# A graph layer kernel: its first matmul on row halves, its scatter on column halves, its bias copied by ScalarE

## What is computed

```python
h = relu(layernorm(x))
xp = h @ lin1_w
C = 0.5 * (cos(edge_weight * PI / 10) + 1)
W = (ssp(edge_attr @ mlp_w1 + b1) @ mlp_w2 + b2) * C[:, None]
msg = xp[src] * W
agg = segment_sum(msg, dst)
x + ssp(agg @ lin2_w + lin2_b) @ lin_w + lin_b
```

## Time and profile before

| | us |
|---|---|
| median of 3 runs | 2164.73 |
| lowest and highest run | 2164.29, 2168.45 |
| span of the profiled execution | 2162.6 |
| TensorE matmuls busy | 1804.4 |
| TensorE weight loads busy | 1331.3 |
| VectorE busy | 1433.5 |
| ScalarE busy | 636.2 |
| GpSimd busy | 1626.7 |

### The profile page before, as it was taken

One profiled execution on the slowest core, in us unless ns is written; L12 is line 12 of the kernel. 1 busy time (PEld: TensorE's weight loads), 2 busy tenths in 40 slices (PEclk: granted clock), 3 DMA queues, 4 the chain that ended last, 5 costly groups with the idle time before them and its releaser, 6 DMA issues.

```text
span 2162.6 us, 28443 instructions
## 1 busy us (share of the span) xinstructions
PE 1804.4 (83%) x8534; PEld 1331.3 (62%) x8535; DVE 1433.5 (66%) x3688; ACT 636.2 (29%) x976; POOL 1626.7 (75%) x1742
## 2 busy tenths in 40 slices
PE   6888888888877888878888888888878888878887
PEld 6556666666655656656665666666656666655665
DVE  7867666666665666666666666666667666666665
ACT  6323232222222222222232222222322223222221
POOL 7877777777777777777777777777777777777775
PEclk9678787687787787887687877777778678788776
DMA  9322222222232222223232222222222222232221
GB/s 286 90 73 69 81 76 75 79 76 81 68 82 81 71 79 81 75 74 82 68 82 79 77 79 70 81 81 68 81 81 75 74 81 76 74 81 76 73 72 47
DMA packets 100170, 175.95 MB, mean 81 GB/s; under 512 B 29163, under 2 KB 67748, under 8 KB 94870
## 3 DMA queue, kind: packets, MB, share of 16 engines
q0 software_dynamic: 53152, 108.91, 18.0%
q1 hardware_dynamic: 46868, 65.22, 11.4%
HBM read 161.21 MB, written 12.80 MB: 80 GB/s over the span
## 4 chain that ended last, share of the span: by engine, by line
POOL 60%; issue 20%; PE 14%; DMA 3%; DVE 2%; DVEq 0%; ACT 0%; POOLq 0%; SPq 0%
POOL XG L307 59%; PE PW L619 4%; PE PA L631 4%; PE PX L605 3%; DMA XG<-xp_scratch,IX 3%; PE PW L617 1%; DVE SCR L403 1%; POOL TB L207 1%; DVE XG L509 1%; PE PF L648 0%; DVE MV L409 0%; PE PF L656 0%; PE PW L586 0%; DMA X<-x 0%; PE PX L573 0%
## 5 line engine op out<-in xcount | busy, mean ns | idle before, releaser
L307 POOL DMA_INDIRECT XG<-xp_scratch,IX x1661 | 1574.8, 948 | 507.4 <-issue 498.3
L371 ACT ACTIVATE TB<-TB 128x512 f32<-128x512 f32 x416 | 261.7, 629 | 1407.0 <-DVE TB L491 1406.9
L619 PEld LDWEIGHTS PW<-W,TB 128*128 128x128 f32 x3322 | 592.2, 251 | 21.4
L619 PE MATMUL PW<-W,TB 128*128 128x128 f32 x3322 | 594.5, 338 | 0.0
L509 DVE TENSOR_TENSOR XG<-PW,XG 128x512 f32<-128x512 f32 x416 | 286.2, 688 | 451.1 <-DMA XG<-xp_scratch,IX 448.1
L605 PE MATMUL PX<-AT,W 50*128 50x512 f32 x832 | 554.8, 752 | 7.1 <-DMA AT<-attr_t 7.1
L631 PEld LDWEIGHTS PA<-OH,XG 128*128 128x128 f32 x3322 | 544.4, 248 | 1.0 <-DVE XG L509 0.5
L631 PE MATMUL PA<-OH,XG 128*128 128x64 f32 x3322 | 543.3, 322 | 0.2 <-DVE AG L517 0.2
L617 PEld LDWEIGHTS PW<-BPB,ones 128*128 128x128 bf16 x416 | 41.3, 99 | 704.4 <-issue 649.6
L617 PE MATMUL PW<-BPB,ones 128*128 128x512 bf16 x416 | 195.2, 469 | 315.4 <-DVE XG L509 314.4
L491 DVE TENSOR_SCALAR TB<-PX,B 128x512 f32<-128x512 f32 x416 | 309.8, 745 | 202.9 <-PE PX L605 200.5
(11 more groups left out here) (73 smaller groups left out, 329.2 us busy)
## 6 DMA issues: line engine op xcount, KB each, us to landing
AT<-attr_t SPq DMA_DIRECT2D x103, 400.0 KB
XG<-xp_scratch,IX POOLq DMA_INDIRECT x1661, 2.5
X<-x SPq DMA_DIRECT2D x12, 512.0 KB, 7.4
xp_scratch<-XG SPq DMA_DIRECT2D x24, 256.0 KB, 4.4
out<-X SPq DMA_DIRECT2D x24, 256.0 KB, 5.2
IX<-src_t SPq DMA_DIRECT2D x1, 830.5 KB, 6.5
CC<-ew_t SPq DMA_DIRECT2D x1, 830.5 KB, 8.4
DI<-dst_t SPq DMA_DIRECT2D x1, 830.5 KB
```

The costliest lines, as they stand in the source:

```text
L307: e.indirect_dma_start(XG[q % XG_N][0:p, k * D:(k + 1) * D], None, xp, bass.IndirectOffsetOnAxis(ap=IX[0:p, t0 + k:t0 + k + 1], axis=0)).t ...
L371: e.activation(T[:, 0:w], T[:, 0:w], ACT.Exp).then_inc(s_ex, 1)
L619: ins = e.matmul(P[0:p, k * D:(k + 1) * D], TB[q % TB_N][:, k * TILE:k * TILE + p], W2[:, :], start=False, stop=(k == n - 1))
```

## The change

- **First layer:** two quads at a time, on even steps. The attributes of even quads lie in partitions 0 to 49 of AT, those of odd quads in partitions 64 to 113, and W1 lies there twice. A 51st row of ones (loaded from `one`) with `b1` in W1 adds the bias. Four matmuls of 256 columns alternate between the rows 0 to 50 and 64 to 114. There are four banks PX instead of three, and one bank PA instead of two. Each AT chunk comes in two DMAs.
- **Softplus:** max(v, 0) + ln(0.5 + 0.5 exp(-|v|)). ScalarE takes |v| from PX, then exp and ln; VectorE needs one operation (L508 of the changed kernel), and the clamp is gone.
- **Second layer:** from the third quad on ScalarE copies the bias, held in BB, into the bank PW (L398), and TensorE adds to it. The copy for quad q waits for the product of q-2 (`s_m`) and stands behind ln of q+1.
- **Compare:** one operation for the four tiles (L517), without the edge factor.
- **Product:** four operations of 128 columns (L536), each waiting for its own gather, each with the edge factor CC.
- **Scatter:** each tile as two matmuls of 64 columns of XG, whose results go to the partitions 0 to 63 and 64 to 127 of PA (L665).
- **Add:** at step i for quad i-4, and ahead of the product of i-3 in VectorE's order. The scatter of q waits for the add of q-1.

```diff
-    XG_N, TB_N, X1_N, OH_N = 6, 4, 3, 3
+    XG_N, TB_N, X1_N, OH_N = 6, 4, 4, 3
...
-        W1 = sb("W1", [NG, D])
+        W1 = sb("W1", [ODD + NG + 1, D])
-        B1 = sb("B1", [128, 2])
+        BB = sb("BB", [128, QT, D])
...
-        AT = [sb(f"AT{i}", [NG, CHQ * QE]) for i in range(AT_N)]
+        AT = [sb(f"AT{i}", [ODD + NG + 1, CHQ // 2 * QE]) for i in range(AT_N)]
...
-        PA = [ps(f"PA{i}") for i in range(2)]
+        PA = ps("PA")
-        PN = PW + PA
+        PN = PW + [PA, PX[3]]
...
+            tables += [(AT[i][r + NG:r + NG + 1, :], one, s_dx) for i in range(AT_N) for r in (0, ODD)]
             for c in range(NNC):
                 keep(c)
                 if c >= 3 and c % 2 and tables:
-                    for _ in range(2):
+                    for _ in range(3):
                         if tables:
                             to, frm, done = tables.pop(0)
                             e.dma_start(to, frm).then_inc(done, 16)
             assert not tables
 
             def load(k):
-                e0 = k * CHQ * QE
-                w = min(CHQ * QE, EDGES - e0)
                 if k >= AT_N:
                     e.wait_ge(s_x1, min(NQ, (k - AT_N + 1) * CHQ))
-                e.dma_start(AT[k % AT_N][:, 0:w], attr_t[:, e0:e0 + w]).then_inc(s_at[k % AT_N], 16)
+                for r in range(2):
+                    A = AT[k % AT_N][ODD * r:ODD * r + NG, :]
+                    if k < NCH - 1:
+                        e.dma_start(A.rearrange("p (j e) -> p j e", e=QE),
+                                    attr_t[:, k * CHQ * QE:(k + 1) * CHQ * QE].rearrange(
+                                        "p (j r e) -> p r j e", r=2, e=QE)[:, r]).then_inc(s_at[k % AT_N], 16)
+                    else:
+                        for j in range(CHQ // 2):
+                            e0 = (k * CHQ + 2 * j + r) * QE
+                            w = min(QE, EDGES - e0)
+                            e.dma_start(A[:, j * QE:j * QE + w], attr_t[:, e0:e0 + w]).then_inc(s_at[k % AT_N], 16)
 
             load(0)
             e.wait_ge(s_x1, 1)
...
             e.preload_act_table_set("natural_log_exp_and_others")
+            e.wait_ge(s_bb, 1)
             for i in range(STEPS):
                 q = i
                 if q < NQ:
                     t0, n, last = quad(q)
                     w = (n - 1) * TILE + last
                     T = TB[q % TB_N]
-                    e.wait_ge(s_cl, q + 1)
-                    e.activation(T[:, 0:w], T[:, 0:w], ACT.Exp).then_inc(s_ex, 1)
+                    e.wait_ge(s_x1, q + 1)
+                    if q >= TB_N:
+                        e.wait_ge(s_w, q - TB_N + 1)
+                    e.activation(T[:, 0:w], PX[q % X1_N][:, 0:w], ACT.Abs).then_inc(s_ab, 1)
+                    e.wait_ge(s_ab, q + 1)
+                    e.activation(T[:, 0:w], T[:, 0:w], ACT.Exp, scale=-1.0).then_inc(s_ex, 1)
                     e.wait_ge(s_ex, q + 1)
                     e.activation(T[:, 0:w], T[:, 0:w], ACT.Ln, scale=0.5, bias=HALF[:, :]).then_inc(s_ln, 1)
+                q = i - 1
+                if 2 <= q < NQ:
+                    t0, n, last = quad(q)
+                    p = last if n == 1 else TILE
+                    e.wait_ge(s_m, q - 1)
+                    e.activation(PW[q % 2][0:p, 0:n * D], BB[0:p, 0:n, :].rearrange("p k d -> p (k d)"),
+                                 ACT.Copy).then_inc(s_pb, 1)
                 if i - 1 in AT_STEP:
                     c = AT_STEP[i - 1]
                     n0, w, _ = nodes(c)
...
-            e.wait_ge(s_bs, 64)
+            e.wait_ge(s_bs, 48)
+            e.tensor_copy(BB[:, :, :], BR[:, 0, 0:1, :].to_broadcast([128, QT, D])).then_inc(s_bb, 1)
...
                     w = (n - 1) * TILE + last
                     e.wait_ge(s_ln, q + 1)
                     T = TB[q % TB_N]
-                    e.scalar_tensor_tensor(out=T[:, 0:w], in0=PX[q % X1_N][:, 0:w], scalar=B1[:, 1:2],
-                                           in1=T[:, 0:w], op0=ALU.add, op1=ALU.max).then_inc(s_h, 1)
-                q = i
-                if q < NQ:
-                    t0, n, last = quad(q)
-                    w = (n - 1) * TILE + last
-                    e.wait_ge(s_x1, q + 1)
-                    if q >= TB_N:
-                        e.wait_ge(s_w, q - TB_N + 1)
-                    e.tensor_scalar(TB[q % TB_N][:, 0:w], PX[q % X1_N][:, 0:w], B1[:, 0:1], CLAMP,
-                                    ALU.add, ALU.min).then_inc(s_cl, 1)
+                    e.scalar_tensor_tensor(out=T[:, 0:w], in0=PX[q % X1_N][:, 0:w], scalar=0.0,
+                                           in1=T[:, 0:w], op0=ALU.max, op1=ALU.add).then_inc(s_h, 1)
                 q = i - 3
                 if 0 <= q < NQ:
                     t0, n, last = quad(q)
                     if q >= OH_N:
                         e.wait_ge(s_sc, q - OH_N + 1)
-                    for k in range(n):
-                        p = last if k == n - 1 else TILE
-                        ins = e.tensor_scalar(OH[q % OH_N][0:p, k, :], WI[0:p, 0:WIN], REL[0:p, t0 + k:t0 + k + 1],
-                                              CC[0:p, t0 + k:t0 + k + 1], ALU.is_equal, ALU.mult)
-                    ins.then_inc(s_oh, 1)
-                    e.wait_ge(s_w, q + 1)
-                    for k in range(n):
-                        e.wait_ge(s_g[q % XG_N][k], 16 * (q // XG_N + 1))
                     p = last if n == 1 else TILE
                     assert n == 1 or last == TILE
-                    G = XG[q % XG_N][0:p, 0:n * D]
-                    e.tensor_tensor(G, PW[q % 2][0:p, 0:n * D], G, ALU.mult).then_inc(s_m, 1)
-                q = i - 5
+                    e.tensor_tensor(OH[q % OH_N][0:p, 0:n, :], WI[0:p, 0:WIN].unsqueeze(1).to_broadcast([p, n, WIN]),
+                                    REL[0:p, t0:t0 + n].unsqueeze(2).to_broadcast([p, n, WIN]),
+                                    ALU.is_equal).then_inc(s_oh, 1)
+                q = i - 4
                 if 0 <= q < NQ:
                     e.wait_ge(s_sc, q + 1)
                     if q:
                         e.wait_ge(s_ac, q)
                     base = e.value_load(BI[0:1, q:q + 1], min_val=0, max_val=NODES - 1)
                     A = AG[:, bass.ds(base, WIN)]
-                    e.tensor_tensor(A, A, PA[q % 2][:, 0:WIN], ALU.add).then_inc(s_ac, 1)
+                    e.tensor_tensor(A, A, PA[:, 0:WIN], ALU.add).then_inc(s_ac, 1)
+                q = i - 3
+                if 0 <= q < NQ:
+                    t0, n, last = quad(q)
+                    p = last if n == 1 else TILE
+                    e.wait_ge(s_w, q + 1)
+                    for k in range(n):
+                        e.wait_ge(s_g[q % XG_N][k], 16 * (q // XG_N + 1))
+                        G = XG[q % XG_N][0:p, k * D:(k + 1) * D]
+                        ins = e.scalar_tensor_tensor(out=G, in0=PW[q % 2][0:p, k * D:(k + 1) * D],
+                                                     scalar=CC[0:p, t0 + k:t0 + k + 1], in1=G,
+                                                     op0=ALU.mult, op1=ALU.mult)
+                    ins.then_inc(s_m, 1)
                 if i == FLAG_STEP:
 
                     link(e.memset(CK[:, NT - 1:NT], 0.0))
...
             e.wait_ge(s_cst, 2)
 
             for i in range(STEPS):
                 q = i
-                if q < NQ:
-                    t0, n, last = quad(q)
-                    w = (n - 1) * TILE + last
+                if q < NQ and q % 2 == 0:
                     k = q // CHQ
-                    e.wait_ge(s_at[k % AT_N], 16 * (k // AT_N + 1))
+                    e.wait_ge(s_at[k % AT_N], 32 * (k // AT_N + 1) + (32 if k == NCH - 1 else 0))
                     if q < X1_N:
                         e.wait_ge(s_re, NNC)
+                        e.wait_ge(s_xe, NNC)
                     else:
-                        e.wait_ge(s_h, q - X1_N + 1)
-                    o = (q % CHQ) * QE
-                    e.matmul(PX[q % X1_N][:, 0:w], W1[:, :], AT[k % AT_N][:, o:o + w], start=True,
-                             stop=True).then_inc(s_x1, 1)
+                        e.wait_ge(s_h, q - X1_N + 2)
+                    o = (q % CHQ) // 2 * QE
+                    _, n, last = quad(q + 1)
+                    w = [QE, (n - 1) * TILE + last]
+                    turns = [(0, 0), (0, 1), (1, 0), (1, 1)] if w[1] == QE else [(0, 0), (1, 0), (0, 1), (1, 1)]
+                    for half, r in turns:
+                        a = half * QE // 2
+                        b = min(a + QE // 2, w[r])
+                        if a < b:
+                            K = slice(ODD * r, ODD * r + NG + 1)
+                            ins = e.matmul(PX[(q + r) % X1_N][:, a:b], W1[K, :], AT[k % AT_N][K, o + a:o + b],
+                                           start=(a == 0), stop=(b == w[r]))
+                            if b == w[r]:
+                                ins.then_inc(s_x1, 1)
                 q = i - 2
```

(21 more changed lines are left out.)

35 lines of the change are left out of this document (20 added, 15 removed).

## The result

The changed kernel takes 2290.49 us, median of 4 runs from 2282.46 to 2300.40, beside 2164.51 us for the kernel before (median of four runs now). The ratio is 1.0583 (1.0554 to 1.0613): slower by 126 us or 5.8%. The sign was forecast, the size was not: the forecast was 2542 us, 378 more than before, three times what came. Only the whole range, 2163 to 2720, which reaches down to rival 1, holds it.

The account below looks back on a forecast made before the run. Gathers bound the kernel at 5.01 us a quad; the ring would take 5.81: 85 + 2417 + 13 + 25 = 2540 us of span, runs' median 2.1 above, forecast 2542 us. Own range 2363 to 2746, whole range 2163 to 2720.

Parts of the forecast that it names:

- rival 1: VectorE, ScalarE and TensorE keep up with the gathers, which still set the end: 2165 us, chance 0.13.
- What bounds the kernel now: GpSimd's gathers, 1.253 us each, 5.01 us a quad; all other engines follow them.
- The ring: Product, bias copy, second layer, scatter, add follow each other across engines in every quad, without overlap: 4.48 us upper, 6.10 lower clock.
- The links: Steps per quad: product 1.05, copy 0.70, layer 0.89 or 1.71, scatter 1.00 or 1.80, register load 0.84 us.
- scatter to its end: 1.00 upper, 1.80 lower, if the halves bring nothing: TensorE's scatter in the ring, taken as no shorter when split into column halves: 1.00 or 1.80 us.
- Rival 2: TensorE's scatter column halves run side by side: scatter 0.5 and 0.9, ring 4.2 and 5.4, 2222 us; chance 0.16.
- I take a quarter of the time at the upper clock: TensorE's clock mix over the ring's two lengths, a quarter upper: 5.81 us a quad.
- the forecast's own 4.7 and 6.3: Ring in us a quad, upper and lower clock, with 0.1 each added for first weight load and change of shape.
- 25 us for the node blocks: The 25 node blocks' layers and adds, in the same queues, 1 us each that no longer hides.
- Rival 4: VectorE's wide compare with two SBUF inputs holds gathers up: at most 0.4 us a quad, 2331 us; chance 0.05.
- Rival 3: Neither row nor column halves run side by side on TensorE: 6.3 us a quad mixed, 2746 us; chance 0.12.
- Small loads, smaller AT pieces, more work for ScalarE at no cost: Loads go into SP's gaps, AT transfers hide behind gather buffers, ScalarE reaches 2.6 of 5.0 us: no time added.

Follow-up runs that it names:

- run 1: Changed kernel with VectorE's add of quad i-4 put behind the product of quad i-3 instead of ahead of it: 2168.94 us, ratio 1.0018 to the kernel before.
- run 3: Changed kernel with the register load of an add's base ahead of the wait for the scatter instead of behind it: 2178.42 us, ratio 1.0060.
- run 4: Changed kernel with the product as one 512-column operation and the compare, with the edge factor, as four narrow ones again: 2166.65 us, ratio 1.0005.
- run 5: Changed kernel with the bias put into PW by TensorE's matmul again and ScalarE's copy left out: 2177.56 us, ratio 1.0050.
- run 6: Kernel before with only the add of quad i-4 ahead of the product of i-3, and with it one bank PA: 2166.10 us, ratio 0.9998.
- run 8: Changed kernel plus six idle matmuls behind the scatter of even steps, where no first layer follows: 2179.14 us, ratio 1.0067.
- run 10: Changed kernel with the add's register load ahead of the wait for the scatter and the compare as four narrow operations: 2163.68 us, ratio 0.9996.
- run 11: Changed kernel with the scatter whole again and the add behind the product: 2174.36 us, ratio 1.0044.
- Run 2: Changed kernel with each tile's scatter as one matmul on all 128 columns again, four a quad: 2719.11 us, ratio 1.2546.
- run 7: Changed kernel plus six idle matmuls behind the scatter of every odd step, where the first layer follows anyway: 2277.56 us, ratio 1.0509.

## Why the prediction was right and wrong

**What bounds the kernel now: right.** The gathers at 5.01 us a quad set the pace before, and every kernel whose ring is open, or short enough, or at the upper clock often enough comes back to them: runs 1, 3, 4, 5, 6, 8, 10 and 11.

**The ring as the cost of the change: right, and shown.** It stands in the chain with all five links, and runs 1, 3, 4 and 5 each open it or shorten another link.

**The links, one by one.** The product was 1.05 and measured 1.26 with the step from the add (0.14 + 1.12): the four parts start 0.26 us apart and not 0.21. The stand-in of the earlier trace rows is another operation, without a pointer scalar; that this is the reason is likely and not tested. The copy with its signals was 0.70 and is 0.77 (0.03 + 0.74). The load was 0.84 and is 0.77. The layer to the scatter's start was 0.89 and 1.71 plus 0.2 for the first weights and the change of shape; it is 1.06 and 1.98, so 0.2 upper and 0.3 lower: the allowance was fair. Run 2 takes its two parts apart, as its whole scatter has the shape of the layer: there the layer to the scatter's start is 1.84 us at the lower clock (1051.18 to 1053.02), and 0.97 at the upper by the median of the trace. So the change of shape costs 0.14 and 0.09 us, and the start behind a wait 0.13 and 0.08. The Trainium skill (TensorEngine Tiling (Array Packing), Tiling Modes, Key Properties) has a drain at each change of mode. The 0.14 and 0.09 us agree with it in kind.

**First failed step: "scatter to its end: 1.00 upper, 1.80 lower, if the halves bring nothing".** They bring 0.31 and 0.68 us: the scatter takes 0.69 and 1.12. Rival 2, which had a chance of 0.16, was the case in kind. The sum with that and the other links is 4.55 and 5.90, where the forecast had 4.7 and 6.3. The halves had been weighed by the absence of a row that shows them. The Trainium skill (TensorEngine Tiling (Array Packing), Tiling Modes, Key Properties) says that tiles load and multiply in parallel. The trace agrees: the 16 half records start in pairs 7 ns apart and take 0.69 us, where 8 whole ones took 1.00.

**Second failed step: "I take a quarter of the time at the upper clock".** A quarter is a mean clock of 0.625, and no row gave it; the span's mean of 0.759 is half of the time at the upper clock. With only one of the two steps put right the forecast is still too high: at the measured 4.55 and 5.90 a quarter gives 5.49 a quad and about 2410 us, and half of the time at the forecast's own 4.7 and 6.3 gives its lower bound, 2363. With both put right it is 5.14 a quad. The intervals' mean is 5.27, as the lower clock falls on the links more than on the rest: the mean scatter is 0.96 us, which is the lower clock for some 60% of it. With the scatter whole the forecast for the same case was 2542, and the chip gave 2719 at a mean clock of 0.56: there the quarter was too much. So the clock mix was not a constant to be chosen once: it differed between two kernels that differ only in the scatter, and lay on either side of the guess. Why it is so much lower with the scatter whole, although TensorE is then busy 72% of the span and not 64%, no run settles; that filling the empty hole brings it up, run 8 shows.

**A term without effect: 25 us for the node blocks "that no longer hides".** The intervals in which TensorE works on node blocks have a mean of 5.15 us, the others 5.30, so no turn is seen to be longer for them.

**Rival 2's own number** was 2222, 68 us under what came. It had the scatter at 0.5 and 0.9, a full halving, and the product 0.2 too short; its quarter of the time at the upper clock erred the other way, so that its nearness is in part luck: with half of the time its 4.2 and 5.4 would be 4.7 a quad, under the gathers' 5.01. **Rival 4** was right in kind: 12 us of gather time in run 10, and not the 166 that its bound allowed; in the changed kernel itself the gathers wait for the scatter, and no run shows that the compare costs it any time. The Trainium skill (SBUF — State Buffer, SBUF: two separate sides) names the lock of the port pair for an operation with two SBUF inputs. The 955 against 948 ns of runs 3 and 10 agree. **Rival 3** was out: both halves of rows run at once, 1.13 and 2.08 us for two quads, as the earlier trace rows for one.

**Small loads, smaller AT pieces, more work for ScalarE at no cost: right.** The first gathers start within 2 us of where they did, and ScalarE's 2.6 us a quad never stand ahead of the copy, which starts 0.03 us after the product's end throughout.

## What to carry to other kernels

Follow one buffer around all engines before counting busy time: a wait that is harmless by itself closes a ring when the step behind it in one queue feeds the step ahead of it in another, and then every link costs in full, an idle register load as much as a matmul. When an edit takes work from TensorE, ask where the holes between its pieces will lie and what stands in each: in this case the second layers behind an empty hole were the slow ones, and the clock granted at the links of the ring counted, not the mean. But work put into a hole pays only while it fits, as run 7 shows. When a ring is found, the cheapest cut is often one step moved in one queue.
